# A top-2-of-8 expert FFN around attention: all experts for every token, or only the chosen rows, sorted through device memory

## The reference

```
x = x + 0.5 * ffn(layernorm(x))
x = x + attention(layernorm(x))      # 16 heads of 8, causal, sequences of 256
x = x + 0.5 * ffn(layernorm(x))      # the same weights again

ffn(x):  scores = softmax(x @ router_w)                 # 8 experts
         sel    = top_k(scores + expert_bias, 2)
         out    = sum over the 2 chosen e of scores[e] * swiglu(x, w1[e], w2[e], w3[e])
         return out + swiglu(x, sw1, sw2, sw3)           # the shared expert
swiglu:  (silu(x @ w1) * (x @ w3)) @ w2                  # all 128 x 128
```

## Time and profile before

| | |
|---|---|
| Three runs | 1344.02, 1347.78 (median), 1349.27 us |
| Profiled execution, own time | 1349.75 us |
| Its span, first to last instruction | 1348.0 us |
| Mean granted TensorE clock | 0.973 |
| Transfers | 11.85 MB, mean 9 GB/s, almost all in the first 35 us |

### The profile page before, as it was taken

One profiled execution on the slowest core, in us unless ns is written; L12 is line 12 of the kernel. 1 busy time (PEld: TensorE's weight loads), 2 busy tenths in 40 slices (PEclk: granted clock), 3 DMA queues, 4 the chain that ended last, 5 costly groups with the idle time before them and its releaser, 6 DMA issues. The chain is left out here.

```text
span 1348.0 us, 34907 instructions
## 1 busy us (share of the span) xinstructions
PE 1238.0 (92%) x11940; PEld 691.8 (51%) x11940; DVE 1107.1 (82%) x2686; ACT 833.5 (62%) x1477; POOL 554.5 (41%) x658
## 2 busy tenths in 40 slices
PE   5999999999979999999999999899899999999998
PEld 2555555555533555555555555555455555555554
DVE  6888888888975688888888888888688898988876
ACT  5665565656543566666666666666565656566564
POOL 3454544544530233333333333333354554554444
PEclk9999999999995799999999999999899999999999
DMA  6000000000000000000000000000000000000000
GB/s 186 2 1 1 0 0 0 0 0 0 1 1 1 1 1 2 2 2 2 2 2 2 1 2 2 1 2 2 2 2 16 9 16 8 16 8 16 8 9 25
DMA packets 21417, 11.85 MB, mean 9 GB/s; under 512 B 960, under 2 KB 21312, under 8 KB 21312
## 3 DMA queue, kind: packets, MB, share of 16 engines
q1 hardware_dynamic: 21312, 10.43, 2.8%
HBM read 6.23 MB, written 4.19 MB: 8 GB/s over the span
## 5 line engine op out<-in xcount | busy, mean ns | idle before, releaser
L672 POOL TENSOR_TENSOR h_lo<-h,h_hi 128x512 f16<-128x512 f32 x288 | 337.7, 1173 | 386.3 <-ACT h_hi L634 375.6
L1109 DVE TENSOR_REDUCE neg_max_at<-score_at 128x2 f16<-128x512 f32 (+1 forms) x384 | 254.4, 692 | 78.1 <-PE score_at L940 72.5
L1229 POOL TENSOR_SCALAR_AFFINE_SELECT probs_at<-probs_at 128x512 f32<-128x512 f32 x256 | 157.0, 637 | 352.4 <-ACT probs_at L1187 351.9
L634 ACT ACTIVATE h_hi<-h 128x512 f16<-128x512 f32 x288 | 180.6, 627 | 152.7 <-DVE h L435 150.8
L1187 ACT ACTIVATE probs_at<-prob_at 128x512 f32<-128x512 f32 x384 | 201.6, 598 | 79.3 <-PE prob_at L972 77.4
L435 DVE TENSOR_TENSOR h<-prod,gate_b 128x512 f32<-128x512 f32 x256 | 174.9, 683 | 53.9 <-PE gate_b L543 53.7
L564 PE MATMUL y_b<-w_hi,h_hi 128*128 128x128 f16 x1152 | 207.8, 219 | 2.6 <-POOL h_lo L672 2.6
L564 PE MATMUL y_b<-w_hi,h_lo 128*128 128x128 f16 x1152 | 207.8, 219 | 0.0
L564 PE MATMUL y_b<-w_lo,h_hi 128*128 128x128 f16 x1152 | 207.8, 219 | 0.0
L429 DVE TENSOR_TENSOR prod<-silu,b 128x512 f32<-128x512 f32 x256 | 175.5, 686 | 37.9 <-ACT silu L623 23.6
L623 ACT ACTIVATE silu<-a 128x512 f32<-128x512 f32 x288 | 169.7, 589 | 49.7 <-PE a L530 48.3
(11 more groups left out here) (138 smaller groups left out, 2203.4 us busy)
## 6 DMA issues: line engine op xcount, KB each, us to landing
x<-in_L_attn_x_dram SPq DMA_DIRECT2D x16, 256.0 KB, 3.0
out_dram<-x SPq DMA_DIRECT2D x16, 256.0 KB, 2.3
raw_w<-in_L_ffn_w_dram SPq DMA_DIRECT2D x3, 512.0 KB, 5.2
raw_w<-in_L_ffn_sw_dram SPq DMA_DIRECT2D x3, 64.0 KB, 4.1
raw_attn<-in_L_attn_W_Q_dram SPq DMA_DIRECT2D x1, 64.0 KB, 4.9
raw_attn<-in_L_attn_W_K_dram SPq DMA_DIRECT2D x1, 64.0 KB, 3.6
raw_attn<-in_L_attn_W_V_dram SPq DMA_DIRECT2D x1, 64.0 KB, 3.6
raw_attn<-in_L_attn_W_O_dram SPq DMA_DIRECT2D x1, 64.0 KB, 3.7
```

The source lines that it names most:

```text
L634: nc.scalar.activation(h_hi[k][:, :], h[k][:, :], ACT.Copy).then_inc(hhi_done, 1)
L672: nc.gpsimd.tensor_tensor(h_lo[k][:, :], h[k][:, :], h_hi[k][:, :], ALU.subtract).then_inc(hlo_done, 1)
L1109: nc.vector.tensor_reduce(dst, src, AX.X, ALU.max, negate=True).then_inc(max_done, 1)
L1229: nc.gpsimd.affine_select(out=p, in_=p, compare_op=ALU.is_ge, fill=0.0, base=0, pattern=[[0, GROUPS], [1, P]], channel_multiplier=-1).then ...
```

## The change

The FFN computes the shared expert for each chunk (16 steps, "S") and, of the routed ones, only the rows that a token chose.

- **Routing (class `Routing`).** Tokens are handled in 4 quarters of 16 tiles. For a whole quarter at once DVE runs 32 steps (`gates`): the choice, and then each chosen row's place in a list sorted by expert, where each expert's rows begin at a multiple of 128. Ranks are counted by 32 small matmuls (`rank`). A quarter has 32 tiles of chosen rows and room for 8 of padding: `PARTS` = 40 parts of 128 rows, computed as `ROUNDS` = 10 rounds of 4 parts ("B"), always all of them.
- **Scatter.** POOL writes each normed tile, with the gate in column 128 of a 132-column f32 row, into the list in device memory, once for each of the two choices: 32 indirect transfers of 128 rows per quarter.
- **Rounds.** SP loads 4 parts of the list (6 loads ahead), PE transposes them, `up` and `down` take the expert's weights at an address from a register (loaded per round by `load_experts`), ACT scales y by the gate and issues the store of the four parts itself (`copy_y`).
- **Fetch.** POOL gathers each token's two result rows with indirect transfers that add to x in SBUF, 128 per FFN.
- **Engines.** h_lo moves from POOL to DVE; the scaling of the FFN's norm moves from DVE to ACT; `a` and `b` have one PSUM bank each instead of two; `LAG` is 2 instead of 3. The FFN loops are written out. In phase 0 the lists are first filled with zeros, 2.7 MB per quarter.
- **Order.** Phase 0: S0 to 11, rounds of quarter 0, S12, 13, quarter 1, S14, 15, quarters 2 and 3. Phase 1: S0 to 3, quarter 0, S12 to 15, quarter 1, S4 to 11, quarters 2 and 3.
- **Beside attention.** 13 chunks' gathers of phase 0, one per unit; the second FFN's norm, router, choice and scatter for quarters 0 to 2 as soon as their chunks leave attention: jobs `U`, `L`, `N` (transpose, logits, ranks), `choose` on DVE, scatters on POOL one per unit, later two. The norms of chunks 0 and 1 for attention move from phase 0 into it.

Core of the diff (`gates`, tables and declarations cut):

```diff
-LAG = 3
+LAG = 2
+QUARTERS = 4
+QUARTER = CHUNKS // QUARTERS
+BATCH = QUARTER * TILES
+PARTS = 2 * BATCH + EXPERTS
+ROUNDS = PARTS // TILES
...
+    def blank_rows(self, sp, rows, q):
+        self.wait_pool_tables(sp)
+        for i in range(PARTS // (2 * TILES)):
+            some = rows["in"][q][i * 2 * TILES * P:(i + 1) * 2 * TILES * P, :]
+            sp.dma_start(some.rearrange("(p t) d -> p t d", p=P),
+                         self.blank[:, :, :]).then_inc(self.blanked[q], DMA)
...
+    def scatter(self, pool, q, first, last):
+        nc, half = self.nc, BATCH // 2
+        if first == 0:
+            pool.wait_ge(self.gate_step, q * GATE_STEPS + PLACED)
+            pool.wait_ge(self.scaled, (q + 1) * QUARTER)
+        for n in range(first, last):
+            k, t = divmod(n, BATCH)
...
+            nc.gpsimd.indirect_dma_start(self.rows["in"][q][:, :],
+                                         bass.IndirectOffsetOnAxis(self.place[:, k, tile:tile + 1], 0),
+                                         self.xn[:, at, :], None).then_inc(
+                                             self.second[q] if k else self.scattered[q][t // half], DMA)
...
+    def fetch(self, pool, c, k, first, last):
...
+        if first == 0 and k == 0 and c % QUARTER == 0:
+            for s in range(STORES):
+                pool.wait_ge(self.row_stored[s], len(range(s, (q + 1) * ROUNDS, STORES)) * DMA)
...
+        for t in range(first, last):
+            tile = c * TILES + t
+            nc.gpsimd.indirect_dma_start(self.x[:, tile, :], None, self.rows["out"][q][:, :],
+                                         bass.IndirectOffsetOnAxis(self.place[:, k, tile:tile + 1], 0),
+                                         compute_op=ALU.add).then_inc(self.fetched[k][c % 2], DMA)
...
+            def up(n):
+                kind, c = work[n]
+                m, hi, lo = source(kind, c)
...
+                    parts = [slice(k * P, (k + 1) * P) for k in range(TILES)]
                 for dst, name, free, done in ((a_bank, "w1", silu_done, a_done), (b_bank, "w3", prod_done, b_done)):
+                    wait_count(pe, free, n)
+                    for k, part in enumerate(parts):
+                        pairs = ((name + "_hi", hi), (name + "_hi", lo), (name + "_lo", hi))
+                        for i, (ws, xs) in enumerate(pairs):
+                            last = nc.tensor.matmul(dst[:, part], weight(ws, n, k), xs[:, part],
+                                                    start=(i == 0), stop=(i == 2))
...
+            def load_experts(n):
+                if n < len(work) and work[n][0] == "B":
+                    q, j = divmod(work[n][1], ROUNDS)
+                    if j == 0:
+                        pe.wait_ge(route.gate_step, (q + 1) * GATE_STEPS)
+                    regs = [pe.alloc_register(f"part{n}_{k}_{phase}") for k in range(TILES)]
+                    pe.load(regs, route.expert[q][0:1, TILES * j:TILES * (j + 1)])
...
+            def copy_y(n):
+                i = work[n][1]
+                act.wait_ge(w2_done, n + 1)
+                if i >= STORES:
+                    act.wait_ge(route.row_stored[i % STORES], i // STORES * DMA)
+                for t in range(TILES):
+                    last = nc.scalar.activation(row_out[i % STORES][:, t, :], y_bank[n % 2][:, t * P:(t + 1) * P],
+                                                ACT.Identity, scale=row_in[i % LOADS][:, t, GATE:GATE + 1])
+                last.then_inc(y_copied, 1)
+                q, j = divmod(i, ROUNDS)
+                act.wait_ge(y_copied, i + 1)
+                act.dma_start(round_rows(rows["out"][q], j),
+                              row_out[i % STORES][:, :, :]).then_inc(route.row_stored[i % STORES], DMA)
...
+            (phase 0, POOL)
+                for c in range(CHUNKS):
+                    route.norm_root(pool, c)
+                    if c == 4:
+                        prepare.low(pool, nc.gpsimd, "w2")
+                    if c == FIRST_SCATTER:                      # 8
+                        prepare.wait_blank(pool, 0)
+                    if FIRST_SCATTER <= c < FIRST_SCATTER + QUARTER:
+                        some = 2 * BATCH // QUARTER
+                        route.scatter(pool, 0, some * (c - FIRST_SCATTER), some * (c - FIRST_SCATTER + 1))
+                for q in range(1, QUARTERS):
+                    prepare.wait_blank(pool, q)
+                    route.scatter(pool, q, 0, 2 * BATCH)
...
+            (phase 1, POOL)
+                route.scatter(pool, QUARTERS - 2, SCATTERED_BEFORE, 2 * BATCH)
+                for c in sorted(normed):
+                    route.norm_root(pool, c)
+                route.scatter(pool, QUARTERS - 1, 0, 2 * BATCH)
+                fetch(0, 0)
+                for c in range(1, CHUNKS):
+                    fetch(c, 0)
+                    fetch(c - 1, 1)
+                fetch(CHUNKS - 1, 1)
...
-PLACES = (((), ("q",), ("k",)), (("o10",), ("o11",), ("Q00",)), (("K00",), ("Q01",), ("K01",)),
-          (("m10", "m11"), ("y1",), ()),
+PLACES = ((("U", "N"), ("q",), ("k",)), (("o10",), ("o11",), ("Q00",)), (("K00",), ("Q01",), ("K01",)),
+          (("m10", "m11"), ("y1",), ("L",)),
...
+            (attention, POOL, in each unit u of turn c)
+                        if exists(c + FETCH_FIRST):             # c + 3
+                            before.fetch(pool, c + FETCH_FIRST, u // TILES, u % TILES, u % TILES + 1)
+                        since = (c - QUARTER - 2) * 2 * UNITS + u - UNITS
+                        q, n = divmod(since, 2 * BATCH)
+                        if 0 <= q < QUARTERS - 2:
+                            route.scatter(pool, q, n, n + 1)
+                        elif q == QUARTERS - 2 and 2 * n < SCATTERED_BEFORE:
+                            route.scatter(pool, q, 2 * n, 2 * n + 2)
```

More of the change, by code:

```diff
@@ L238, in ffn_phase @@
+def ffn_phase(nc, x, consts, w, rows, route, phase, x_dram, out, prepare=None):
     with ExitStack() as ctx:
@@ L246, in sem @@
             return ctx.enter_context(nc.semaphore(f"{name}_{phase}"))
[L248 to L256, removed]
+        ident = consts["ident"]
+        keep = 2 * QUARTER
+        xt_hi = sb("xt_hi", [P, keep, CHUNK], F16)
+        xt_lo = sb("xt_lo", [P, keep, CHUNK], F16)
+        again = None if phase == 0 else [sb(f"again{s}", [P, TILES, P], F32) for s in range(2)]
+        rt_hi = [sb(f"rt_hi{s}", [P, CHUNK], F16) for s in range(2)]
+        rt_lo = [sb(f"rt_lo{s}", [P, CHUNK], F16) for s in range(2)]
         silu = [sb(f"silu{s}", [P, CHUNK], F32) for s in range(2)]
-        prod = sb("prod", [P, CHUNK], F32)
         h = [sb(f"h{s}", [P, CHUNK], F32) for s in range(3)]
@@ new lines, in ffn_phase @@
+        place_of = {s: n for n, s in enumerate(work)}
+        turns = []
+        turns_at = {}
+        for s in range(len(steps)):
+            here = [("R" if c in normed else "T", c) for c in range(CHUNKS) if turned[c] == s]
+            if s + 2 < len(steps) and steps[s + 2] and steps[s + 2][0] == "B":
+                here.append(steps[s + 2])
+            turns_at[s] = here
+            turns += here
+        turn_no = {t: m for m, t in enumerate(turns)}
+        router_at = {turned[c] + 1: c for c in normed}
@@ L459, in _ @@
+            batches = sorted(first_gate.values())
             if prepare:
                 prepare.dve_consts(dve)
[L461 to L472 removed]
@@ new lines, in _ @@
+            for s in range(len(steps)):
+                n = s - lead
+                if n >= 0:
+                    silu_a(n)
+                for t in turns_at[s]:
+                    split_x(turn_no[t])
+                if n >= 0:
+                    split_h(n)
+                if s in first_gate:
+                    route.exponents(act, first_gate[s])
+                if s in normed_at:
+                    route.norm_scale(act, normed_at[s])
+                if s in again_at:
+                    scale_again(again_at[s])
+                if prepare and s == 1:
+                    prepare.high(act, "router")
+                if prepare and s == 2:
+                    prepare.high(act, "w1")
+                if prepare and s == 3:
+                    prepare.high(act, "w3")
+                    prepare.high(act, "w2")
+                if prepare and s == 4:
+                    prepare.high(act, "attn", y_bank[1])
+                if n >= LAG and work[n - LAG][0] == "B":
+                    copy_y(n - LAG)
```

980 lines of the change are left out of this document (624 added, 356 removed).

## The result

The changed kernel takes 1365.03 us (1363.36 to 1367.59, 4 runs) against 1348.53 us (1344.02 to 1355.71, 4 runs) of the kernel before on the same chip: a ratio of 1.0105, 95% interval 1.0066 to 1.0143. It is slower by 1%; I had forecast 1150 us. The profiled execution's span is 1361.7 us, where the steps of the prediction sum to 1154.

What follows compares the result with a forecast made beforehand. It took the FFN as bound by TensorE's columns and attention by nearly full TensorE, VectorE and ScalarE. Phases of 284 + 616 + 254 = 1154 us of span, plus 2 around it, gave a forecast of 1150 us, range 1050 to 1310.

Steps and rivals of the forecast that it cites:

- T: Time one indirect transfer keeps POOL busy: 1.2 us, ends 0.2 and 3.0; forecast wrong if over 1.4.
- the granted clock: TensorE's clock, 1.00 and 0.99 in the FFN phases, 0.94 in attention: said to decide nothing.
- VectorE's added work in attention: Statistics, logits, choosing and ranks add 51 us on VectorE; 38 show, bounds 10 and 60; VectorE above 85%.
- Last phase: Second FFN: rounds with choosing 200 us, then POOL's last 32 gathers until 249, landing and output store 5: 254 us.
- Rival 1: POOL's queue bounds all phases, last phase 47 + 160T; T 1.4 to 1.8 chance 0.10, above 1.8 and slower 0.09.
- Attention: Middle phase, 572 us before: two norms +6, VectorE's added work +38, POOL hidden at T = 1.2: 616 us.
- First phase: First FFN: first shared step near 30 us, some 17 us stall behind scatters, then rounds and choosing: 284 us.
- The step with a norm: Shared-expert step that also norms and takes logits, priced as VectorE's sum: 3.8 us.
- The blank rows: First phase: the first quarter's 2.7 MB of zeros stand ahead of x chunks 5 to 15: 10 us.
- A round: Four 128-row parts in either FFN, ScalarE's sum 3.2 us: about 3.4 us, bounds 3.0 to 4.8.
- rival 2: Register addresses bind TensorE in the rounds: a round at 4.7 us, +100, total 1250 us; chance 0.12.
- The register addresses: Weights addressed through registers on TensorE, 24 a round: 0 to 2.4 us, 1.0 taken as showing.

Runs made afterwards that it cites:

- e1: The changed kernel with gathers that overwrite x instead of adding to it; 1587.08 us, ratio 1.1714 to the kernel before.
- e4: The changed kernel without the 104 gathers in attention and the 96 scatters there and at the last phase's start; 1465.81 us, ratio 1.0803 to the kernel before.
- e9: The changed kernel with one-column memsets replacing VectorE's choosing steps for three quarters in attention; 1322.73 us, ratio 0.9736 to the kernel before.
- e7: The changed kernel with the norm statistics taken one step ahead; 1492.75 us, ratio 1.1044 to the kernel before.
- e10: Hybrid: the changed kernel's routed first phase, statistics one step ahead, gathers in attention, last FFN phase as before the change; 1305.04 us, ratio 0.9602 to the kernel before.
- e6: The changed kernel with the first quarter's blank rows moved behind the loads of x; 1529.10 us, ratio 1.1313 to the kernel before.
- the four groups: Sixteen follow-up kernels, mostly edits of the changed kernel, measured four at a time, each group on one chip with the kernel before (1352.13 to 1354.46 us where given).
- e5: The changed kernel unedited, measured again; 1520.57 us, ratio 1.1211 to the kernel before.
- e16: The kernel of e10 with a 128x256 fill ahead of each scatter; 1356.27 us, ratio 1.0044 to the kernel before.
- e14: The kernel of e10 unedited, measured a second time, on a chip with the gaps; 1419.17 us, ratio 1.0488 to the kernel before.
- e12: The changed kernel with statistics one step ahead and a 128x256 fill ahead of all scatters; 1385.08 us, ratio 1.0195 to the kernel before.
- e8: The changed kernel with a 128x512 fill ahead of each scatter of the first phase; 1465.11 us, ratio 1.0839 to the kernel before.
- e11: The kernel of e10 with a 128x512 fill ahead of each scatter of the first phase; 1350.64 us, ratio 0.9977 to the kernel before.

## Why the prediction was wrong

**The step that failed: "POOL issues 128 scatters and 128 gathers per FFN ... I take T = 1.2", one T for both kinds.** The scatter is 1.26 us, close to it. The gather that adds is 1.84, beyond the T of 1.4 that the text named as its limit; e1 shows that the addition makes the difference. A second step failed beside it: the granted clock, of which the prediction says that "it decides nothing here", and VectorE's added work in attention, of which it let 38 us show.

- *Last phase, 254 forecast, 346 measured.* Rival 1's own formula with the two prices, 47 + 32 x 1.26 + 128 x 1.84, is 323, and the places came later: its scatters start at 1077.6, 62 us into the phase instead of 42. That makes 343. The mechanism was rival 1's (POOL's queue is the bound), to which I gave 0.09 and which I priced by one T with a turning point at 1.8; the mean T of both kinds is 1.55, yet the total is slower than before. The stretch of rounds itself ended 240 us after the start, not 200.
- *Attention, 616 forecast, 698 measured.* "POOL ... hidden at T = 1.2, not above 1.3": a gather is above. By the marks attention gained 138 us (720 against 582). Taking all transfers out gives back 55 (e4), taking choosing out 50 (e9), and norm, turn and router are what is left, some 33; 17 of these stand at the edges (in e4 attention's first job stands 14.7 us behind the first mark and its last one 13.4 ahead of the second, 4.8 and 6.4 in the kernel before). I had 44 for everything, 6 for the norms and 38 of the 51 us of added VectorE work; what is not POOL's cost 83. The busy time was forecast well (503 us, measured 508), but as a share it is 73% and not over 85%: a full VectorE was not the mechanism. Choosing comes in bursts, TensorE waits behind them, and its clock falls, to which I had put nothing: 10.3 us of choosing stretch a turn by 15.7 in the worst case, with the clock at 1.2 GHz for two thirds of that turn. From mark to mark the granted clock went from 0.94 to 0.85, and TensorE's busy time from 521 to 595 us for 4% more matmuls. In e4 it is 0.91 and in e9 0.92, so the share of each holds some of the clock's; how much is its own was not separated. The split comes from one profile per kernel, on different chips, where the unedited attention alone varies by 26 us, and no run takes out both parts at once to show that they add; I take it to be good to some 10 us.
- *First phase, 284 forecast, 318 measured.* The first S was to start near 30 us and its first matmul came at 39.2, its product at 45.8. I had also misread the start before: the matmul at 18.24 is that of the second step, the first one was at 13.3. The first round was reached at 154, by my sum at 127. The step with a norm was priced as VectorE's sum, 3.8 us; it is the chain VectorE, POOL, ScalarE, TensorE of 6 to 8 us shown above. e7 wins back 10 us at the start and 18 at the end (last product 302.3 in e10 against 320.0 in e9, same chip). The blank rows, to which I had put 10 us, cost nothing (e6). A round was 3.6 to 3.8 us, 3.4 forecast: with 40 rounds that is the rest.
- *Right*: the price of a round within some 0.2 to 0.4 us (rival 2 had 4.7), the scatter's price, the length of choosing, and that the scatters between the norms of chunks 8 to 12 hold all engines: steps of 11 to 14 us from 71 to 121 us. The register addresses cost less than the 1.0 us a round that I took: the 24 matmuls that use them as weights start about 0.078 us apart, where the other 12 have 0.056, which makes some 0.5 us.
- *Neither forecast nor rival*: on three of the five occasions (the result and the four groups) the changed kernel loses up to another 155 us to the gaps. The result was taken without them. That is luck: nothing in the prediction provided for them.

The Trainium skill (SBUF — State Buffer, SBUF: two separate sides) had the writing of descriptors locked out beside a VectorE copy, 3.1 us instead of 0.62. That does not show here: gathers take 1.54 us in the last 100 us with VectorE idle and 1.57 on average over the kernel, and none takes over 2 us.

## What to carry to other kernels

Price an indirect transfer by kind before a design rests on hundreds of them, and count what the issuing engine does in each phase: here 512 of them are 128 x 2 x (1.26 + 1.84) = 794 us of one engine, against 260 taken off TensorE and 284 off VectorE. Move work to sit beside a full phase only after asking how bursty it is, and look at the granted clock behind it: 10.3 us of choosing stretched one turn by 15.7, and attention gave back 126 us where both FFN phases had won 112. A change may be good in one part and bad in another: the routed first phase alone, with the last one left as it was, is 4% faster where the whole change is 1% slower.

## What was not expected of the hardware

Long runs of back-to-back indirect transfers that don't add (1.25 to 1.26 us apart) can nearly stop the other engines, for as long as the run lasts (80 us for 64 scatters). The window from 160 to 225 us, in the run of the result and in e5:

```profile
160.00:225.00 65.00, 51.47 (x624) 43.14 (x624) 41.55 (x91) 39.03 (x97) 50.21 (x56) 0.95 0.57 151
```
```profile
160.00:225.00 65.00, 8.17 (x29) 3.37 (x30) 1.94 (x5) 0.00 (x0) 49.60 (x58) 0.50 0.16 52
```

TensorE mostly starts a matmul 0.7 to 2.8 us after the one before, VectorE does 5 instructions and ScalarE none. At 1.46 us apart some three quarters of the loss is gone (e16 against e14 and e12), at 1.67 us nearly all of it but the fill's own time (last product at 371.0 in e8; at 345.2 in e11 on the gap-free chip, with e7's edit, which is worth some 18), and adding gathers at 1.84 us never show it. It was there in the first, second and fourth group and absent in the third and in the result, always alike for all kernels of a group; the four groups ran on four chips, so chip and occasion can't be told apart. What the engines lack in that time is open: the transfer engines are at a share of 0.16, and the records of TensorE name no semaphore, queue or operand. Against the addressing of weights through a register speaks that the transposes `xt` and the other two engines, which use none, are held as well. The Trainium skill (Runtime: NRT & Kernel Launch, Instruction fetch mechanics) has instructions fetched in blocks of 256. The transfers of instructions in e5 from 157 to 234 us speak against these as the cause:

```profile
q8 instruction: 1, 0.02, 0.1%
q14 instruction: 1, 0.01, 0.0%
```

These are one block of 16 KB and one of 8 KB in 77 us, while TensorE does 35 matmuls and pauses ahead of nearly each.
